# Graph kernel on one Trainium2 core: GpSimd copies the index columns of half a ring at a time

## What is computed

```python
h = relu(layernorm(x)); x = x + L0(h)   # attention, 4 heads: xl[src] + xr[dst], softmax over edges of a node
h = relu(layernorm(x)); x = x + L1(h)   # out = seg_sum(w * s[col], row) + seg_sum(w * s[row], col)
h = relu(layernorm(x)); x = x + L2(h)   # twice: seg_sum(x[src]) @ W_msg + x @ W_self
h = relu(layernorm(x)); x = x + L3(h)   # attention, 8 heads, scores s_u[src] + s_v[dst]
```

## Time and profile before

| what | value |
|---|---|
| time, median of 3 runs | 10797.18 us (10796.2 to 10806.08) |
| the profiled execution: its time | 10752.12 us |
| the profiled execution: its span | 10750.4 us |
| GpSimd busy | 5855.2 us, 54% of the span |
| TensorE busy | 6331.9 us, 59% |
| VectorE busy | 5005.6 us, 47% |
| ScalarE busy | 1331.9 us, 12% |
| mean granted TensorE clock | 0.739 of 2.4 GHz |

### The profile page before, as it was taken

How to read it: one execution, slowest core, us unless ns; L and a number is a source line. 1 busy time by engine, 2 the same in 40 slices (tenths; PEclk the granted TensorE clock), 3 DMA queues, 4 the chain that set the end, 5 groups by cost and what they waited for, 6 DMA issues and landing times. The chain is left out here.

```text
span 10750.4 us, 137753 instructions
## 1 busy us (share of the span) xinstructions
PE 6331.9 (59%) x24674; PEld 4941.0 (46%) x24675; DVE 5005.6 (47%) x12212; ACT 1331.9 (12%) x3940; POOL 5855.2 (54%) x5805
## 2 busy tenths in 40 slices
PE   4888875757466666555554555555555642222575
PEld 2888864546344444433333444444444442222454
DVE  6555558885444444355553222242222321114888
ACT  2222211213222222100001000010000300000000
POOL 3777740000288888777775777747777167763000
PEclk9898878988777777676766777677777655555798
DMA  4666674541377777644433222222222166663454
GB/s 147 189 190 187 186 231 152 169 136 35 69 104 105 104 104 105 111 134 137 133 117 91 82 82 82 82 75 81 83 83 83 41 193 204 201 193 99 129 170 155
DMA packets 835068, 1358.92 MB, mean 126 GB/s; under 512 B 112279, under 2 KB 488661, under 8 KB 834981
## 3 DMA queue, kind: packets, MB, share of 16 engines
q0 software_dynamic: 315328, 634.04, 26.7%
q1 hardware_dynamic: 385684, 562.46, 16.0%
q10 hardware_dynamic: 133968, 161.50, 4.8%
HBM read 943.05 MB, written 414.50 MB: 126 GB/s over the span
## 5 line engine op out<-in xcount | busy, mean ns | idle before, releaser
L1012 POOL DMA_INDIRECT rows_in<-table,gather_rows x2352 | 2500.5, 1063 | 1034.2 <-issue 511.1
L1103 PE MATMUL ps_p<-rows_in,hot 128*128 x5280 | 2000.5, 542 | 1584.6 <-SPq L976 1328.8
L1103 PEld LDWEIGHTS ps_p<-rows_in,hot 128*128 128x128 f32 x5280 | 1360.3, 271 | 2180.1 <-issue 1928.7
L1722 POOL DMA_INDIRECT scatter_sums<-regionC,idx x880 | 1387.3, 1576 | 307.1 <-issue 246.0
L956 DVE TENSOR_TENSOR regionC<-regionC,ps_p 128x257 f32 (+2 forms) x1320 | 558.6, 423 | 1767.9 <-DVEq L953 1569.1
L1464 PE MATMUL ps_p<-regionA 128*128 128x265 f32 (+1 forms) x3520 | 969.4, 435 | 426.0 <-DVE regionC L956 194.4
L1464 PEld LDWEIGHTS ps_p<-regionA 128*128 128x128 f32 x3520 | 735.3, 214 | 659.8 <-DVE regionC L956 239.3
L1012 POOL DMA_INDIRECT regionB<-table,gather_rows x784 | 848.4, 1082 | 344.5 <-issue 272.2
L1012 POOL DMA_INDIRECT regionC<-table,gather_rows x784 | 817.1, 1042 | 296.7 <-issue 265.1
L1927 PE MATMUL psS<-dst_scores,regionA 128*128 x1760 | 393.4, 362 | 793.7 <-issue 385.4
L1927 PEld LDWEIGHTS psS<-dst_scores,regionA 128*128 128x128 f32 x1760 | 383.7, 330 | 803.4 <-issue 803.4
(11 more groups left out here) (303 smaller groups left out, 8011.7 us busy)
## 6 DMA issues: line engine op xcount, KB each, us to landing
regionA<-edge_rows SPq DMA_DIRECT2D x880, 256.0 KB, 3.2
edge_rows<-regionB SPq DMA_DIRECT2D x196, 512.0 KB
edge_rows<-regionC SPq DMA_DIRECT2D x392, 256.0 KB
regionC<-srcrow_d SPq DMA_DIRECT2D x220, 256.0 KB
scatter_sums<-zero_rows ACTq DMA_DIRECT2D x8, 6400.0 KB, 42.3
regionA<-scatter_sums ACTq DMA_DIRECT2D x49, 1024.0 KB
rows_in<-table,gather_rows POOLq DMA_INDIRECT x2352
regionB<-rrow_d ACTq DMA_DIRECT2D x110, 256.0 KB
```

The source lines that it names most:

```text
L1012: g.indirect_dma_start(out=rows_of(b * per + j), out_offset=None, in_=table, in_offset=bass.IndirectOffsetOnAxis(ap=rows[j], axis=0), boun ...
L1103: x = te.matmul(ps[(u.c * VG + j) % NB][:, 0:width], hot[:, b, 2 * j + k, :], at_tile(G, slot[j] * 2 + k), start=k == 0, stop=k == 1)
L1722: g.indirect_dma_start(out=scat, out_offset=bass.IndirectOffsetOnAxis(ap=idx[:, b, j:j + 1], axis=0), in_=sums[:, b, j, :], in_offset=None ...
```

## The change

GpSimd no longer waits and copies for each group. At the first group of each half of the ring it waits for all the slots of that half, copies the index columns of all its groups with one copy and waits for it; then it issues the indirect DMAs of the half one after another. The last piece of a pass may be shorter. `gather_rows` keeps its size, with the half as its middle dimension. A half is 4 groups of 4 tiles in `attention_fetch0`, 3 groups of 4 in the plain passes and 3 groups of 8 in `attention_fetch3`. SP releases a group 2 groups behind the one that has landed, in all five passes.

```diff
--- before.py
+++ after.py
@@ -965,7 +965,7 @@
             v.sem_inc(s_add.sem, nbank)
 
         def landed_groups(sp, s_rows, used, unused, ring, keep=None, kept=None):
-            behind = ring // 2
+            behind = 2
             regs = registers(sp, 'by_visit', 1)
 
             def group(u):
@@ -993,24 +993,27 @@
                 sp.wait_ge(ring_free[b], 1)
                 sp.sem_inc(ring_free[b], -1)
 
-        def index_columns(g, u, ring, per, idx):
-            b = u.c % ring
-            g.tensor_copy(idx[:, b, :], gidx[:, bass.ds(u.val * per, per)]).then_inc(own_p, 1)
-            g.wait_ge(own_p, 1)
-            g.sem_inc(own_p, -1)
-            return [idx[:, b, j:j + 1] for j in range(per)]
-
         def gather(g, table, rows_of, s_rows, ring, per, free, idx):
             top_row = g.to_reg(NP - 1)
+            half, groups = (ring // 2, ET // per)
+
+            def indices(u):
+                n = half if not isinstance(u.val, int) else min(half, groups - u.val)
+                for b in range(u.c % ring, u.c % ring + n):
+                    g.wait_ge(free[b], 1)
+                    g.sem_inc(free[b], -1)
+                g.tensor_copy(idx[:, u.c % ring // half, 0:n * per], gidx[:, bass.ds(u.val * per, n * per)]).then_inc(own_p, 1)
+                g.wait_ge(own_p, 1)
+                g.sem_inc(own_p, -1)
 
             def fetch(u):
                 b = u.c % ring
-                g.wait_ge(free[b], 1)
-                g.sem_inc(free[b], -1)
-                rows = index_columns(g, u, ring, per, idx)
+                if b % half == 0:
+                    indices(u)
                 for j in range(per):
-                    g.indirect_dma_start(out=rows_of(b * per + j), out_offset=None, in_=table, in_offset=bass.IndirectOffsetOnAxis(ap=rows[j], axis=0), bounds_check=top_row, oob_is_err=True).then_inc(s_rows[b].sem, 16)
-            for t_ in turns(g, ET // per, ring, 0):
+                    at = b % half * per + j
+                    g.indirect_dma_start(out=rows_of(b * per + j), out_offset=None, in_=table, in_offset=bass.IndirectOffsetOnAxis(ap=idx[:, b // half, at:at + 1], axis=0), bounds_check=top_row, oob_is_err=True).then_inc(s_rows[b].sem, 16)
+            for t_ in turns(g, groups, ring, 0):
                 fetch(t_.at(0))
 
         def plain_pass(name, table, acc, acc_flat, width, weighted, fold=None, own=None):
@@ -1018,7 +1021,7 @@
             s_rows = rows_count(name, RG)
             with ExitStack() as ctx:
                 G = sb('rows_in', [P, RG * EG, width], F32, ctx)
-                idx = sb('gather_rows', [P, RG, EG], I32, ctx)
+                idx = sb('gather_rows', [P, 2, RG // 2 * EG], I32, ctx)
                 hot = sb('hot', [P, 2, GS, P], F32, ctx)
                 wgt = sb('step_weights', [P, S], F32, ctx) if weighted else None
                 ps = [bank(f'ps_p{i}', ctx) for i in range(NB)]
@@ -1228,7 +1231,7 @@
             row_free = [sem(f's_row_free{b}') for b in (0, 1)]
             with ExitStack() as ctx:
                 feat = sb('feat', [P, 2, 2 * D], F32, ctx)
-                idx = sb('gather_rows', [P, RG0, EG], I32, ctx)
+                idx = sb('gather_rows', [P, 2, RG0 // 2 * EG], I32, ctx)
                 featT = sb('featT', [P, 2, 4, P], F32, ctx)
                 psX = [bank(f'psX{b}', ctx) for b in (0, 1)]
                 psF = [bank(f'psF{b}', ctx) for b in (0, 1)]
@@ -1867,7 +1870,7 @@
             read3 = [sem(f's_slot_read3{b}') for b in range(R3)]
             with ExitStack() as ctx:
                 psS = [bank(f'psS{b}', ctx) for b in (0, 1)]
-                idx = sb('gather_rows', [P, R3, GS], I32, ctx)
+                idx = sb('gather_rows', [P, 2, R3 // 2 * GS], I32, ctx)
                 with phase() as block:
 
                     @block.sync
@@ -1887,7 +1890,7 @@
                             sp.sem_inc(free3[b], 1)
                         for b in range(R3):
                             sp.sem_inc(free3[b], 1)
-                        behind = R3 // 2
+                        behind = 2
                         for t_ in turns(sp, NG3, R3, behind):
                             if t_.has(0):
                                 keep(t_.at(0))
```

## The result

| | before | changed |
|---|---|---|
| median of 4 runs, us | 10799.4 (10796.2 to 10806.1) | 11259.0 (11246.6 to 11274.3) |
| span of the profiled execution, us | 10750.4 | 11272.5 |
| granted clock of it | 0.739 | 0.720 |

The ratio is 1.0425, interval 1.0407 to 1.0443: slower by 4.25%. The prediction said 10436 us, with 10540 as its upper end, and gave 0.93 to faster. In four later sessions the same change, with its waits on register values bounded, took 10220 to 10238 us beside 10696 to 10718 for the kernel before; in the last session a kernel that had taken 10222 us took 11179 us, from the same source.

A forecast was written before the change was run, and what follows sets the result against it. GpSimd's issue stream was taken to bound four gather passes, `attention_fetch3` being doubtful. Terms -103 - 273 + 5 + 10 = -361 us took 10797.2 to 10436 us; range 10365 to 10540.

The forecast's parts named there:

- TensorE follows ... the cover is thin.: `attention_fetch0`: TensorE needs 2.43 us per visit, GpSimd will ask for one each 2.61 us; 7% to spare, nothing lost.
- 8 us early: `attention_fetch0`: the slots of the next half are free 8 us before GpSimd wants them, so no wait.
- rival 2: `attention_fetch0`: TensorE becomes the bound as the low clock takes more time; the 103 us are lost, 10539 us; chance 0.06.
- Rival 4: Nothing happens: 12 to 24 DMAs in a row hit their own limit, the gap returns between DMAs; 10797 us; chance 0.03.
- Rival 3: Halves not free in time: each plain-pass half loses 1.6 us, `attention_fetch0` 44 us, `attention_fetch3` 100; 11253 us; chance 0.04.
- The late landing of the earlier trace: `l1`: a group sometimes lands 5.0 us after its last DMA, so the half waits about 0.7 us; 5 us taken.
- +10: `attention_fetch3`: 12 us longer first wait, 43 us saved on copies, 41 us of added waits: 10 us more.
- I expect the stretch to move to the DMAs that now stand there: Four passes without `attention_fetch3`: a copy's extra length passes to the DMAs, so a removed copy saves 0.70 us.
- this term of the sum, 376 us: Copies removed: 103 us less in `attention_fetch0`, 273 us less in `l1`, `l2a` and `l2b`, at 0.70 us each.
- the 41 us of added waits for the shorter lead: `attention_fetch3`: GpSimd's lead over VectorE falls from 6 groups to 4; a quarter of 161 us of waits taken.
- the prediction's low end, 31 less: `attention_fetch3`: 31 us less if VectorE catches up and no waits are added; the other end was 130 more.
- Width costs nothing that shows: Remaining copies: 12 to 24 columns wide instead of 4 or 8, taken as zero cost, at most 28 us.

The follow-up runs named there:

- e0_before_bounded: The kernel before with bounds added to its three waits against register values, nothing else changed: 10721.6 us, ratio 1.0004 to the unaltered kernel before.
- e0_after_again: The changed kernel with its three waits on register values bounded, measured again at another time: 10228.4 us, ratio 0.9555 to the kernel before.
- e0_after_last: The same file as x2_same_length, run at a sixth time: 11179.0 us, ratio 1.0376 to the kernel before.
- x2_same_length: The changed kernel with VectorE's and TensorE's waits masked instead of added to and the landed count starting from zero each pass: 10221.6 us, ratio 0.955.

## Why the prediction was wrong

**"TensorE follows ... the cover is thin."** This is the step that failed under the conditions of the result, together with **"8 us early"** for the half in `attention_fetch0`. I took the pace of the visits (2.43 us) from the trace of before, where GpSimd paused for 1.1 us after every four DMAs. In the result a visit took 1716 / 440 = 3.9 us, the half was late 47 times, and the pass lost 466 us. What the prediction left out is that the other engines' pace could depend on how densely the DMAs are issued; why it does at such times stays open. The granted clock fell to 0.73, from 0.88, after TensorE had been kept waiting: around the timeline above it was busy for 1.29 and 0.20 us of the two stretches of 2 us from 1008, with 1.00 granted, and the next two were granted 0.63 and 0.50. At other times the pass had 0.93, as the prediction asked. My rival 2 had the right place, but the wrong engine: TensorE wasn't the bound by its own work, it stood idle for 0.86 and 2.42 us before the matmuls of the timeline above. Rival 4 asked whether longer runs of DMAs meet a limit of their own; at such times something of the kind shows, but in the other engines and not between the DMAs (idle time before them fell to 267.9 us), and I priced it at no gain instead of a loss.

**Rival 3** came out at 11253 us, and that is chance. It had every half of the plain passes lose 1.6 us; `l2a` and `l2b` got faster by 60 and 53 us in the result, and `attention_fetch0`, whose 466 us decided, it had lose 44.

What I could have seen: the rows of eight DMAs in `attention_fetch3` are where the trace of before has SyncE's register operations of over 0.3 us, 183 of 781 (35 of 790 in `attention_fetch0`, 1 to 3 of 441 in the plain passes), and e0_before_bounded has none. The 12.05 us a group of rival 4, where 11.2 us was the pace, was the second sign: e0_before_bounded takes 1139 / 98 = 11.6. I read neither as a sign that long rows of DMAs slow the others. The late landing of the earlier trace rows is none: the trace of e0_before_bounded has a gap of 3.02 us on TensorE at the same place in `l1`.

**The terms under the other conditions** (e0_before_bounded against e0_after_again, first to last gather DMA, us):

| term | predicted | measured |
|---|---|---|
| `attention_fetch0` | -103 | 1242 to 1126: -116 |
| `l1` | -86 | 1184 to 1083: -101 |
| `l2a` | -91 | 1244 to 1128: -116 |
| `l2b` | -91 | 1247 to 1128: -119 |
| `attention_fetch3` | +10 | 1138 to 1106: -33 |
| sum | -361 | -485 |

What the prediction wanted to see is there: 280 copies, idle time before the DMAs of `attention_fetch0` down by 77 us (0.52 us for each of 147 copies), a granted clock of 0.93, no waits in the plain passes. The mechanism holds, and two sizes are off. "I expect the stretch to move to the DMAs that now stand there" is wrong. In `l2a` the mean DMA got shorter, 1.091 to 1.071 us, or 16 us over 784, and the copy's own stretch went as well: the price is 0.78 to 0.91 us in the four passes where I took 0.70; this term of the sum, 376 us, measured 452. In `attention_fetch3` the 41 us of added waits for the shorter lead never came, which leaves the prediction's low end, 31 less, beside 33 measured. Its only wait for a half is the first, 26.1 us, where I had 16.7 + 12 = 28.7. "Width costs nothing that shows" was right: 73 copies of 48 to 96 columns take 296 ns on average, 441 of 8 to 16 columns 266. With the ratio of these sessions, 0.955, even this gain lies beyond the range I gave, which ended at 10365 / 10797 = 0.960.

## What to carry to other kernels

A small GpSimd operation that the queue waits for ahead of its next DMA cost 0.8 us here, of which 0.7 are the wait and not the work: gather indices in as few copies as the buffers allow. A gain of some per cent that rests on denser DMAs must be measured at several times, each beside the kernel before: here one program was 4.5% faster at one time and 3.8% slower at another. Before the cause of a loss is looked for in the code, compare what should be constant in both traces, the longest register operation and the number of recorded landings.

## What the runs showed of the hardware

- The same program on one core had two levels of time, 9.4% apart, each steady within 0.3% over a session: 10211 to 10222 us and 11154 to 11183 us. The kernel before had them 0.6% apart (10699 and 10766). What sets the level is open; I tried semaphore events (11 to 12 more per us in `attention_fetch0`) and 1 MB of DMA traffic per four visits. Neither brought slow register operations about; the events cost 1.5 to 5.4% of the recorded landings.
- At the upper level of time half of the landings are missing from the record, and register operations of 18 to 150 ns take up to 1.6 us on SyncE and 1.4 us on VectorE and TensorE: 1252 such operations over 0.3 us in e0_after_last, one in x2_same_length. The DMA packets take the same time at both levels. That lost records and stalled engines come together suggests that the way by which events are recorded is what fills up. The Trainium skill (NOTIFIC — the notification-queue block, section "Overflow: three behaviours, one of which stalls the engine") says that the block's internal pipeline always holds its producers back rather than lose a record inside. By that an engine could stall where many events are written at once, but the block itself would lose none of them, so the rule answers for the stalls at most and not for the losses. The traces show both together; no run here shows the block itself, and none compares a time with recording and without.
- Semaphore updates on ScalarE that are recorded with 17 ns mostly stand 67 to 78 ns apart when issued back to back.
